# Row sums of squares in four column groups, and an earlier gather, in the scan stage of a language-model block

## The reference

```
h = table[x]                                   # rows of 256, 32 x 512 tokens
h = h + bimamba(layernorm(h))                  # the scan stage
h = h + moe_block(layernorm(h))                # attention, then 8 experts
```

```
u, z = split(n @ Win.T)                        # 512 channels each
uc = silu(conv4(u) + convb)
dt, B, C = split(uc @ Wx.T)                    # 16, 32, 32
dt = softplus(dt @ Wdt.T + bdt)
state = exp(dt * A) * state + dt * uc * B      # along the 512 tokens
y = (sum(state * C) + uc * D) * silu(z)
o = y @ Wout.T                                 # 256 per token
o = (o - mean(o)) / sqrt(var(o) + eps) * g + b # what the change is about
```

## Time and profile before

| | |
|---|---|
| median of 3 runs | 3888.03 us (3886.52 to 3889.06) |
| profiled execution | 3887.42 us, its span 3885.9 us |
| busy, of the span | PE 94%, PEld 69%, DVE 86%, ACT 76%, POOL 62% |
| mean granted TensorE clock | 0.981 of 2.4 GHz |
| scan stage | about the first 2200 us |

### The profile page before, as it was taken

How to read it: one execution, slowest core, us unless ns; L and a number is a source line. 1 busy time by engine, 2 the same in 40 slices (tenths; PEclk the granted TensorE clock), 3 DMA queues, 4 the chain that set the end, 5 groups by cost and what they waited for, 6 DMA issues and landing times. The chain is left out here.

```text
span 3885.9 us, 70521 instructions
## 1 busy us (share of the span) xinstructions
PE 3666.1 (94%) x19212; PEld 2676.2 (69%) x19213; DVE 3356.2 (86%) x6582; ACT 2940.4 (76%) x4862; POOL 2417.7 (62%) x2145
## 2 busy tenths in 40 slices
PE   5999999999999999999999699999996899999998
PEld 3666666666666666666666377777775788888887
DVE  6999999999999999999999489998996566666665
ACT  5899999999999999999999577777774444444444
POOL 3556566666666666666565657877776455555555
PEclk8999999999999999999999899999997999999999
DMA  4444454445454545455555322222222555555555
GB/s 109 82 88 91 88 92 89 91 88 92 90 96 90 96 90 94 92 92 94 89 90 90 81 69 91 94 95 91 95 91 104 114 96 96 95 94 98 86 97 84
DMA packets 235375, 358.07 MB, mean 92 GB/s; under 512 B 25985, under 2 KB 163586, under 8 KB 235266
## 3 DMA queue, kind: packets, MB, share of 16 engines
q0 software_dynamic: 130288, 215.02, 32.2%
q1 hardware_dynamic: 101536, 139.53, 13.5%
q10 hardware_dynamic: 3442, 2.21, 0.2%
HBM read 121.07 MB, written 168.49 MB: 75 GB/s over the span
## 5 line engine op out<-in xcount | busy, mean ns | idle before, releaser
L641 PE MATMUL pj<-xt,win 128*128 128x512 f32 x3144 | 828.4, 413 | 31.7 <-DVE uc L834 24.7
L641 PEld LDWEIGHTS pj<-xt,win 128*128 128x128 f32 x3144 | 584.2, 190 | 222.6 <-DVE uc L834 55.7
L2037 POOL DMA_INDIRECT out<-e_y,e_to x272 | 470.8, 1731 | 367.9 <-ACT e_y L2143 308.2
L834 DVE SCALAR_TENSOR_TENSOR uc<-pj,convw,uc 128x511 f32<-128x511 f32 (+2 forms) x780 | 516.8, 728 | 5.7 <-ACT uc L420 5.7
L690 PE MATMUL po<-yz,wout 128*128 128x512 f32 x1024 | 473.3, 605 | 39.0 <-ACT fb L510 39.0
L322 POOL TENSOR_TENSOR wk<-v,uc 128x512 f32<-128x512 f32 x260 | 325.6, 1285 | 281.2 <-DVE v L882 280.4
L2088 PE MATMUL e_p<-e_w,e_a 128*128 128x256 f32 x3264 | 416.2, 284 | 0.8 <-DVE e_a L2198 0.8
L2088 PEld LDWEIGHTS e_p<-e_w,e_a 128*128 128x128 f32 x3264 | 393.7, 188 | 11.1 <-DVE e_a L2198 2.3
L2076 PE MATMUL e_p<-e_xt,e_w 128*128 128x512 f32 x1632 | 395.2, 397 | 4.1 <-DVE e_xt L2190 2.4
L690 PEld LDWEIGHTS po<-yz,wout 128*128 128x128 f32 x1024 | 184.0, 189 | 276.5 <-issue 275.8
L2076 PEld LDWEIGHTS e_p<-e_xt,e_w 128*128 128x128 f32 x1632 | 303.2, 189 | 74.9 <-issue 5.8
(11 more groups left out here) (244 smaller groups left out, 8540.0 us busy)
## 6 DMA issues: line engine op xcount, KB each, us to landing
qq<-uc POOLq DMA_DIRECT2D x128, 512.0 KB, 5.5
e_x<-expert_in SPq DMA_DIRECT2D x138, 260.0 KB, 2.6
bb<-bc SPq DMA_DIRECT2D x65, 512.0 KB, 5.7
h_rows<-fb POOLq DMA_DIRECT2D x64, 512.0 KB, 10.8
h_rows<-g SPq DMA_DIRECT2D x34, 512.0 KB, 5.9
h_rows<-cvec POOLq DMA_DIRECT2D x33, 512.0 KB, 12.2
a_h<-h_rows SPq DMA_DIRECT2D x128, 128.0 KB
out<-a_bs SPq DMA_DIRECT2D x128, 128.0 KB
```

What stands on the lines that cost most here:

```text
L641: i = mm(pj[m][:], win[d][wp][:, k, c:c + P], xt[xp][:, k, :], start=(k == 0 and n == 0), stop=(k == KD - 1 and n == 2))
L834: stt(uc[d][:, m, to], pj[m][:, of], convw[d][:, m, tap:tap + 1], uc[d][:, m, to], ALU.mult, ALU.add).then_inc(S["cv"], 1)
L2037: pool.indirect_dma_start(out=out, out_offset=bass.IndirectOffsetOnAxis(ap=to[n][:, j:j + 1].bitcast(U32), axis=0), in_=y[n][:, j, :], in_ ...
```

## The change

The row squares swap their operands. A block of 32 columns of ones is the weights, `sq[:, k, block]` (128 columns) streams, and block `j` goes to the column group `j` of the array, so that its sums land in the 32 partitions `32 j` to `32 j + 31` of `pss[:, 0:128]`, 32 times the same. The loop over `k` is now the outer one. Two steps are new: `row_mean` on ScalarE divides and adds `eps` for the whole 128 x 128 block into `rows2`, and `turn_squares` on TensorE transposes `rows2` into `pss[:, 128:256]`. `row_var` then copies every 32nd of these columns, four in all, into `r2`. `row_mean` stands ahead of the softplus's second absolute value, `turn_squares` between the first half of the u projection and `dead_sums`. On GpSimd the gather of the first direction moves ahead of `row_scale`. Some semaphores are merged into others; `fusion` waits for the squares (`sq_ok`) alone, which come after the copies.

```diff
                     if d == 0:
                         add_bias(s + 1)
+                        gather(s + 2)
                     else:
                         ln_scale(s + 2)
                     if not (first and d == 0):
                         row_scale(t - 1)
-                    if d == 0:
-                        gather(s + 2)
                     scan_inputs(t + 1, 1 - d)
...
             def row_var(t):
-                act.wait_ge(S["ss_ps"], t + 1)
+                act.wait_ge(S["rt_ps"], t + 1)
                 if not (isinstance(t, int) and t == 0):
                     act.wait_ge(S["rr_ok"], t)
-                act.activation(r2[:], pss[:, 0:TT], ACT.Identity, bias=eps[:], scale=1.0 / DM).then_inc(S["rv_ok"], 1)
+                act.activation(r2[:], pss[:, P:2 * P:P // TT], ACT.Copy).then_inc(S["rv_ok"], 1)
+
+            def row_mean(t):
+                act.wait_ge(S["ss_ps"], t + 1)
+                act.activation(rows2[:], pss[:, 0:P], ACT.Identity, bias=eps[:], scale=1.0 / DM).then_inc(S["rc_ok"], 1)
...
-                    act.activation(fo[:, k, :], po[k][:], ACT.Copy).then_inc(S["fo_ok"], 1)
+                    act.activation(fo[:, k, :], po[k][:], ACT.Copy)
...
                     softplus_exp(t + 1, (0,))
+                    if not (first and d == 0):
+                        row_mean(t - 1)
                     softplus_abs(t + 1, (1,))
...
             project_copies(2 * NSEQ - 1, range(KD))
+            row_mean(2 * NSEQ - 1)
             row_var(2 * NSEQ - 1)
...
-                for j in range(TT):
-                    for k in range(KD):
-                        i = mm(pss[:, j:j + 1], sq[:, k, j * P:(j + 1) * P], ones[:, 0:1],
+                group = P // TT
+                for k in range(KD):
+                    for j in range(TT):
+                        i = mm(pss[j * group:(j + 1) * group, 0:P], ones[:, 0:group], sq[:, k, j * P:(j + 1) * P],
                                start=(k == 0), stop=(k == KD - 1))
                 i.then_inc(S["ss_ps"], 1)
+            def turn_squares(t):
+                pe.wait_ge(S["rc_ok"], t + 1)
+                nc.tensor.transpose(pss[:, P:2 * P], rows2[:], ident[:]).then_inc(S["rt_ps"], 1)
...
             def fusion(t, d, halves=range(2)):
-                pe.wait_ge(S["fo_ok"], KD * (t + 1))
                 pe.wait_ge(S["sq_ok"], KD * (t + 1))
...
                 in_proj(t + 1, 1 - d, 0, range(2))
+                if back > 1:
+                    turn_squares(t - 2)
                 dead_sums(t, d)
...
             row_squares(2 * NSEQ - 1, True)
+            turn_squares(2 * NSEQ - 1)
```

More of the change, by code:

```diff
@@ L124, in mamba_stage @@
         r2 = sb("r2", [P, TT])
+        rows2 = sb("rows2", [P, P])
         r3 = sb("r3", [P, TT])
@@ L145, in mamba_stage @@
           d0_ok dt_ok dtu_ok tp_ok da_ok h_ok hc_ok q_ok du_ok mix0 mix1 yv_ok yz_ok xm_ok qd_ps gt_ok ct_ok cnt_ps
-          fl_ok s_ps o_ps fo_ok sq_ok ss_ps rv_ok rr_ok f_ps fin_ok h1_st acc gt2 e_bc e_da e_tp e_h e_hc e_y""".split()
+          fl_ok s_ps o_ps sq_ok ss_ps rc_ok rt_ps rv_ok rr_ok f_ps fin_ok h1_st acc e_bc e_da e_tp e_h e_hc e_y""".split()
         S = {n: sem("m_" + n) for n in names}
@@ L281, in ln_scale @@
             def ln_scale(s):
-                wait_apart(pool, S["st_ok"], s + 1)
+                wait_apart(pool, S["st_ok"], 2 * s + 2)
                 if not (isinstance(s, int) and s == 0):
@@ L810, in ln_stats @@
                     i = nc.vector.bn_stats(stats[:, j, :], g[:, j, :])
-                i.then_inc(S["gt2"], 1)
-                wait_apart(dve, S["gt2"], s + 1)
+                i.then_inc(S["st_ok"], 1)
+                wait_apart(dve, S["st_ok"], 2 * s + 1)
                 for j in range(TT):
@@ L1124, in attention_stage @@
         B = [ctx.enter_context(nc.psum_tensor(f"a_pb{i}", [P, SEQ], F32)) for i in range(4)]
-        names = """c0 ld_w ld_h0 ld_h1 ld_h2 ld_h3 st1 rq1 core_ok root_ok step_ok t1_ps lt_ok qk_ps qk_ok v_ps v_ok s_ps mx_ok
-          sub_ok ex_ok su_ok rc_ok p_ok pt_ps pt_ok av_ps ao_ok pr_ps hh_ok bs_ok st2 ve2 rr2 x2_ok t2_ps x2t_ok
+        names = """c0 ld_w ld_h0 ld_h1 ld_h2 ld_h3 st1 rq1 core_ok root_ok t1_ps lt_ok qk_ps qk_ok v_ps v_ok s_ps red
+          sub_ok ex_ok rc_ok p_ok pt_ps pt_ok av_ps ao_ok pr_ps hh_ok bs_ok st2 ve2 rr2 x2_ok t2_ps x2t_ok
           lg_ps lg_ok st_b rt rk_ps od_ok scat ld_e tab tot_ok seq counted few_ok kept_ps plan_ok zst hi_ok low_ok""".split()
@@ L1277, in scales1 @@
                 pool.tensor_tensor(root[:], ve[:, 1, :], rs1[:, 1, :], ALU.mult).then_inc(S["root_ok"], 1)
-                pool.wait_ge(S["root_ok"], c + 1)
+                pool.wait_ge(S["root_ok"], 2 * c + 1)
                 pool.tensor_tensor(step[:, c * TT:(c + 1) * TT], root[:], rs1[:, 0, :], ALU.mult
-                                   ).then_inc(S["step_ok"], 1)
+                                   ).then_inc(S["root_ok"], 1)
             def scales2(c):
@@ L1704, in less_max @@
                     dve.wait_ge(S["s_ps"], 4 * c + n + 1)
-                    nc.vector.tensor_reduce(mx[:, 4 * i:4 * i + 4, :], each, AX_X, ALU.max).then_inc(S["mx_ok"], 1)
-                    dve.wait_ge(S["mx_ok"], 4 * c + n + 1)
+                    nc.vector.tensor_reduce(mx[:, 4 * i:4 * i + 4, :], each, AX_X, ALU.max).then_inc(S["red"], 1)
+                    dve.wait_ge(S["red"], 8 * c + n + 1)
                     after(dve, "pt_ps", 4 * c)
@@ L1715, in sums @@
                     nc.vector.tensor_reduce(sm[:, 4 * i:4 * i + 4, :], ss[:, 4 * i:4 * i + 4], AX_X, ALU.add
-                                            ).then_inc(S["su_ok"], 1)
-                    dve.wait_ge(S["su_ok"], 4 * c + n + 1)
+                                            ).then_inc(S["red"], 1)
+                    dve.wait_ge(S["red"], 8 * c + n + 5)
                     nc.vector.reciprocal(rs[:, 4 * i:4 * i + 4, :], sm[:, 4 * i:4 * i + 4, :]).then_inc(S["rc_ok"], 1)
@@ L1722, in add_projection @@
                 dve.wait_ge(S["core_ok"], TT * (c + 1))
-                dve.wait_ge(S["step_ok"], c + 1)
+                dve.wait_ge(S["root_ok"], 2 * c + 2)
                 for n, i in enumerate((1, 0)):
```

## The result

The changed kernel takes 3897.58 us (median of 11 runs, 3895.9 to 3902.63); the one before takes 3886.3 us on the same chip (11 runs, 3883.4 to 3889.17). The ratio is 1.0029, interval 1.0021 to 1.0037: the change costs 0.29%, where 3877 us and "faster" had been forecast. The profiled execution of after took 3897.58 us as well.

A forecast was written before the change was run, and what follows sets the result against it. VectorE bounds the 65.95 us pair, nearly abreast of the TensorE/ScalarE chain (1.10 us slack); 0.56 gained less 0.21 leaves 0.35 us x 31 = 10.9 us, with 0.2 lost at the end: 3877 us, 8-in-10 range 3870 to 3894.

The forecast's parts named there:

- the squares in the second direction: Row squares on TensorE: the saving from 1.84 to 1.0 us only lengthens the wait for the output scale there.
- The rivals that ended slower: Column groups not side by side, 3902 us, and gathers holding VectorE, 3988 us; together 0.13.
- the groups do run side by side: Rival on TensorE's row squares: column groups don't overlap, 1.84 us plus 0.38 for regrouping, 3902 us; chance 0.11.
- the gathers held no product of VectorE: Rival in the scan stage: moved gathers keep VectorE's products from their operands, up to 3.8 us a pair, 3988 us; chance 0.02.
- The steps that were forecast: Scan stage: 0.56 us gained on VectorE less 0.21 for the second chain, 0.35 us a pair, 10.9 us over 31.
- The scans lost their 0.56 us: VectorE's four scans of a slot: 5.11 to 4.55 us, as earlier gathers let GpSimd's products end before the scan.
- 17.4 was the most: Gathers moved ahead of the row scale: at most 0.56 us in 31 pairs, 17.4 us; at least nothing.
- the 0.43 and 1.84 of the bounds: New row squares on TensorE: 0.43 us if four groups overlap fully, 1.84 us being the old time.
- the 1.0 taken: New row squares on TensorE: 1.0 us assumed for the 16 passes.
- The row mean was 0.25 as taken: Extra ScalarE step out of PSUM, 128 x 128: 0.25 us, between 0.14 and 0.39.
- The additions to ScalarE's path: Row mean and wait for the turn: 0.50 us in the first direction, 0.25 in the other, 0.75 a pair.
- VectorE's wait for the low half: VectorE's wait for the low half of the next input, 0.8 us a pair: to grow by about 0.2 us.
- the two theories: For the squares without the move: clock falls behind the longer wait, 18 to 22 us slower; or gather at fault, about 0.

The follow-up runs named there:

- the kernel with the early state sum alone: The changed kernel with the state sum moved ahead of the first half of the output projection: 3869.08 us, 0.9955 of the kernel before.
- the last kernel: The changed kernel with the state sum ahead of the output projection and ScalarE's copy of the next input ahead of the first softplus step: 3859.52 us, 0.9931.

## Why the prediction was wrong

**The step that failed** is that of the squares in the second direction: "in the other it becomes a longer wait for the output scale. It matters only if it is not there." The wait did come: of the 1.84 - 0.65 = 1.19 us saved, 1.08 stand ahead of the output projection (1.76 for 0.68). But waiting on TensorE was costed at nothing, and it is not nothing: in 10 of 23 pairs the clock falls to half behind it, and 8 passes take 1.70 us longer. These 1.70 us come on the chain of TensorE and ScalarE, which had no slack left, so the pair grows by all of it. No rival had the clock in it. The rivals that ended slower were wrong: the groups do run side by side, and the gathers held no product of VectorE.

**The sum with it.** The steps that were forecast give 65.95 - 65.63 = 0.32 us a pair, 9.9 us over 31; the falls take 13 x 1.70 = 22 us. That is 12 us slower; 11.3 were measured. The removal of the falls gives the same: without them the kernel takes 3874.83 (three times the squares) or 3875.17 (eight passes more), and 3877 had been forecast.

**The steps that held.** The scans lost their 0.56 us in every pair, for the reason given; the gathers alone give 17.3 us where 17.4 was the most. The gathers did not hold VectorE, as the full gain of their move shows. Nearly all of them kept the lengths they had before: the last one shown took 1.84 us, for 0.95 to 2.17; two of 92 between 400 and 1900 us took 2.9 and 3.2. The squares took 0.64 us, between the 0.43 and 1.84 of the bounds and nearer to the low end than the 1.0 taken. The row mean was 0.25 as taken. The additions to ScalarE's path came to 0.65 us for 0.75: from the copy of the step sizes to the row step was 1016.58 - 1008.59 = 7.99 us before and 1021.87 - 1013.48 = 8.39 after, 0.40, and 0.25 in the other direction. VectorE's wait for the low half grew by 1.02 - 0.78 = 0.24 us in the pairs without a fall.

**A combination that the prediction did not look at.** The two parts were costed one by one. The squares without the move are worth -35 us, not the 18 to 22 us of loss, or none, that the two theories expected, since the later row chain and its longer row scale take the gathers with them.

**What stays open** is why the fall comes in some pairs and not in others behind the same stretch (at 985.09 and not at 1051.96 in the same kernel, with 1.89 and 1.90 us of wait; in after two or three pairs apart, every second pair in the four shown). No run here varied the moment at which a wait comes and left its length. Nor does any run show how much the short passes inside the stretch (`dead_count`, the state sum) count: with the state sum in it, 1.88 us had no fall in the kernel with the early state sum alone, and 2.13 us had two in the last kernel.

## What to carry to other kernels

In this kernel, time saved on TensorE that turned into waiting was not free: look at how long the stretches become in which TensorE has little to do, and read the granted clock behind them. If a wait must grow, put work into it that has to be done anyway (the state sum here, one line moved, took 28.5 us off the changed kernel) before shortening anything ahead of it. And cost the parts of a change together with what each does to the due time of the other.

## What the runs showed of the hardware

The clock and the wait just ahead of the output projection, over the stage of a run: no fall behind 0.68, 0.90, 1.53 and 1.57 us (nor behind 1.38 ahead of the z projection); falls in 10 of 23 pairs behind 1.76, and in 6 of 23 behind 1.89. But with the row squares alone it falls behind 1.00 and 0.50 us parted by two short passes, and in the last kernel twice behind 0.96 with the state sum ahead of it, so the one wait is not the whole condition. Each fall ends within the projection behind it and costs that 1.70 us (5.39 for 3.69; 8.83 for 7.13). The Trainium skill, TensorE: Matmul & The Clock Gate, HAM oscillation — how this bites in real kernels, tells of a kernel whose waits between bursts of matmuls send it back to the half clock each time; the trace agrees that the half clock follows waiting (0.50 behind 1.76 us), and differs in that only part of the pairs are hit.

Four column groups run fully side by side: 16, 24, 32 and 48 passes of 128 columns took 0.64, 0.86, 1.08 and 1.52 us, 0.027 us for each further pass, a quarter of the 0.108 that a quarter of a 512-column pass (0.43) makes. The Trainium skill, TensorEngine Tiling (Array Packing), Key Properties, says that tiles of one mode work in parallel; these four durations agree.

A scan issued while a GpSimd product still reads SBUF stands still for nearly all of what is left of it: 0.56 us in four scans before, 1.80 us (6.35 - 4.55) with the products 1.9 us late.
